# Where the maxima of the FP4 down weight are taken, where the first LoRA factors are split, and a rounding factor moved into a product

## The reference

```
x = x + norm(x) @ (weight * blockmask).T                     # 512 x 512, fp32
x = x + norm(x) @ (int4 weight * scale).T + bias             # 512 x 512
z = norm(x)                                                  # NF4 block with LoRA (rank 16), FI = 1792
  x1 = z + o((q(z) + k(z) + v(z)) / 3)
  x  = x + x1 + down(silu(gate(x1)) * up(x1))                # each weight: NF4[codes] * scales + B @ A
z = norm(x)                                                  # NVFP4 block, 1376 features
  h = silu(fp4(z) @ fp4(gate).T) * (fp4(z) @ fp4(up).T)
  x = x + fp4(h) @ fp4(down).T * mlp_output_scale + z @ lr_A @ lr_B

def fp4(w):                                                  # after a permutation of the channels
    s  = max(max(abs(w)) / (448 * 6), 1e-12)                 # one scale of the whole tensor
    sb = clip(max over 16 of abs(w / s) / 6, 1e-12, 448)     # one scale of each block of 16
    return sign(w) * fp4_level(abs(w / s / sb)) * sb * s     # the last 128 channels pass unquantized
```

## Time and profile before

| | |
|---|---|
| median of 3 runs | 788.04 us (787.42 to 793.67) |
| profiled execution, its own time | 790.65 us |
| its span | 789.3 us |
| its mean granted TensorE clock | 0.972 |
| TensorE busy | 704.4 us (89%) |
| VectorE busy | 555.6 us (70%) |
| ScalarE busy | 447.5 us (57%) |
| GpSimd busy | 219.2 us (28%) |

### The profile page before, as it was taken

How to read it: one execution, slowest core, us unless ns; L and a number is a source line. 1 busy time by engine, 2 the same in 40 slices (tenths; PEclk the granted TensorE clock), 3 DMA queues, 4 the chain that set the end, 5 groups by cost and what they waited for, 6 DMA issues and landing times.

```text
span 789.3 us, 10753 instructions
## 1 busy us (share of the span) xinstructions
PE 704.4 (89%) x3832; PEld 528.2 (67%) x3832; DVE 555.6 (70%) x1065; ACT 447.5 (57%) x579; POOL 219.2 (28%) x208
## 2 busy tenths in 40 slices
PE   1798766897999999999998998988999999989998
PEld 1465433575777766667675676765777789967886
DVE  6879986555577678798798975668543534487883
ACT  3767868576778687886776712354432211244552
POOL 1004100003355546647477564211401000000000
PEclk9999977898999999999999999999999999989999
DMA  9636578786557677676775211201301111100001
GB/s 348 193 116 202 187 236 263 237 282 221 173 168 252 187 243 261 214 248 200 245 220 176 105 37 34 61 28 40 107 26 38 26 38 39 53 1 14 27 27 41
DMA packets 55541, 110.79 MB, mean 140 GB/s; under 512 B 9904, under 2 KB 20560, under 8 KB 55232
## 3 DMA queue, kind: packets, MB, share of 16 engines
q1 hardware_dynamic: 42912, 80.28, 31.5%
q0 software_dynamic: 4384, 14.09, 6.1%
q10 hardware_dynamic: 8192, 15.73, 5.8%
HBM read 92.19 MB, written 17.89 MB: 139 GB/s over the span
## 4 chain that ended last, share of the span: by engine, by line
PE 49%; DVE 20%; ACT 10%; DMA 8%; issue 8%; SPq 3%; ACTq 1%; POOL 0%; DVEq 0%; POOLq 0%
PE bank L1246 13%; PE bank L1247 13%; PE bank L1248 13%; ACT hot L1668 3%; DMA rep<-codes 3%; DMA wide_buf<-in_down_flat 2%; DVE x L2035 2%; DVE hot L1924 2%; PE bank L1360 2%; PE bank L1558 1%; ACT c L1628 1%; DVE bank L1950 1%; DVE q_a L1999 1%; DVE stats L1845 1%; SPq L2328 1%
## 5 line engine op out<-in xcount | busy, mean ns | idle before, releaser
L1668 ACT ACTIVATE hot<-rep,levels 128x2048 f16<-128x2048 f16 x94 | 192.9, 2092 | 24.5 <-DMA rep<-codes 14.7
L1246 PE MATMUL bank<-zt_h,w_h 128*128 128x512 f32 (+1 forms) x232 | 93.7, 404 | 3.2 <-DVE zt_l L2023 2.0
L1248 PE MATMUL bank<-zt_h,w_l 128*128 128x512 f32 (+1 forms) x232 | 91.3, 394 | 0.0
L1247 PE MATMUL bank<-zt_l,w_h 128*128 128x512 f32 (+1 forms) x232 | 91.3, 393 | 0.0
L1246 PE MATMUL bank<-w_h,xq_h 128*128 128x512 f32 (+1 forms) x192 | 74.0, 385 | 2.2 <-ACT xq_l L1760 1.9
L1247 PE MATMUL bank<-w_l,xq_h 128*128 128x512 f32 (+1 forms) x192 | 71.9, 374 | 0.0
L1248 PE MATMUL bank<-w_h,xq_l 128*128 128x512 f32 (+1 forms) x192 | 71.8, 374 | 0.0
L1360 PE MATMUL bank<-hot,diag 128*32 128x512 f16 x856 | 60.7, 394 | 9.2 <-ACT hot L1668 8.4
L2179 POOL TENSOR_TENSOR q_a<-q_a,q_m 128x384 f32<-128x384 f32 (+3 forms) x34 | 35.8, 1052 | 69.9 <-DVE q_m L1809 69.8
L1924 DVE TENSOR_SCALAR hot<-rep,levels 128x2048 f16<-128x2048 f16 x56 | 52.3, 933 | 4.0 <-DMA rep<-codes 3.9
L1962 DVE TENSOR_TENSOR w_l<-bank,w_h 128x512 fp32r<-128x512 f32 x46 | 31.7, 689 | 31.8 <-ACT w_h L1676 31.5
(11 more groups left out here) (221 smaller groups left out, 1676.5 us busy)
## 6 DMA issues: line engine op xcount, KB each, us to landing
rep<-codes SPq DMA_DIRECT2D x56, 512.0 KB, 5.3
...
raw<-in_codes_gu_t ACTq DMA_DIRECT2D x14, 512.0 KB, 4.9
...
raw<-in_codes_attn_t ACTq DMA_DIRECT2D x7, 512.0 KB, 4.3
raw<-in_codes_down_t ACTq DMA_DIRECT2D x7, 512.0 KB, 6.3
...
wide_buf<-in_gate_flat SPq DMA_DIRECT2D x5, 512.0 KB, 5.4
```

Source lines behind the costliest of these rows:

```text
L1246: PE.matmul(psum, lh, rh, start=first, stop=False, **kw)
L1247: PE.matmul(psum, lh, rl, start=False, stop=False, **kw)
L1248: return PE.matmul(psum, ll, rh, start=False, stop=last, **kw)
L1668: S.activation(hots[plan.slot[hot_ring(t), (t, m)]][:], codes_in_place(t), ACT.Relu, bias=levels[:, at:at + 1], scale=levels[:, at + 1:at ...
```

## The change

- **Maxima of down.** The generator of the maxima is split: `gm_steps("early")` takes gate and up where all 18 were taken before, with its own last reduction and its own maximum over the partitions. `gm_steps("down")` (eight steps: one for the first two loads, six reductions, one for the last reduction) runs inside `fp4_weights`, between the rounding of chunk 1 and that of chunk 2 of up, in `wide_buf`, which is free from the last transpose of up's chunk 1 on. The first gather of down, which was asked for one chunk earlier, comes behind it and waits for its last reduction. `gm_clamp` is done once for gate and up and once for down.
- **The rate** of the FP4 side goes from 0.8 to 0.88.
- **The first LoRA split**, `stacks(0)`, moves from ahead of the planes of the first tile to behind those of the third.
- **The factor** 1 + 2^-22 behind each reciprocal is taken out there, and applied in the product that uses the reciprocal: `scalar_tensor_tensor(out, src, TIES_UP, reciprocal, mult, mult)` in place of `tensor_tensor(out, src, reciprocal, mult)`, for the weights, x and h.

The diff, cut to its core:

```diff
@@ -183,11 +184,13 @@
 ATT_RATE = 1.0
 NF4_RATE = 0.86
 MAX_RATE = 1.0
-FP4_RATE = 0.8
+FP4_RATE = 0.88
 CHUNKS = [(f, min(512, FF - f)) for f in range(0, FF, 512)]
 PER = FF * D // P
 GM_PARTS = [(c, min(2 * D, PER - c)) for c in range(0, PER, 2 * D)]
 GM_ALL = [(name, i) for name in ("gate", "up", "down") for i in range(len(GM_PARTS))]
+GM_RANGES = {"early": (0, 2 * len(GM_PARTS)), "down": (2 * len(GM_PARTS), 3 * len(GM_PARTS))}
+GM_COLUMNS = {"early": slice(0, 2), "down": slice(2, 3)}
 HN = NT // 2
 AHEAD = tuple((NG - 1, n) for n in range(HN, HN + 3))
 SCALED_AT = {(0, 0): (0, 1), (0, 2): (1, HN), (HN - 1, 0): (HN, NT)}
...
@@ -420,7 +423,6 @@
         cast(1)
         ship(1)
         fetch(2)
-        stacks(0)
         hits(0)
         yield
         tiles = 2 * len(jobs)
...
@@ -442,6 +444,8 @@
             low_parts()
             if t + 1 < tiles:
                 hits(t + 1)
+            if t == 1:
+                stacks(0)
             if t and u == 0:
                 if i > 1:
                     stacks(i - 1)
...
@@ -474,26 +478,30 @@
 
     ready_nf4 = ready_batches()
 
-    def maxima():
-
-        p.add("idx")
-        p.sends("idx_in", "idx", 3)
+    def gm_steps(part):
+        n0, n1 = GM_RANGES[part]
 
         def load(n):
-            if n < len(GM_ALL):
+            if n < n1:
                 p.add("gm_load", *GM_ALL[n])
                 p.sends(f"wide_in{n % 2}", ("gm", *GM_ALL[n]))
 
-        load(0)
-        load(1)
+        load(n0)
+        load(n0 + 1)
         yield
-        for n in range(len(GM_ALL)):
-            if n:
+        for n in range(n0, n1):
+            if n > n0:
                 load(n + 1)
             p.add("gm_max", *GM_ALL[n])
             yield
-        p.add("gm_all")
+        p.add("gm_all", part)
         yield
+
+    def maxima():
+
+        p.add("idx")
+        p.sends("idx_in", "idx", 3)
+        yield from gm_steps("early")
 
     def fp4_weights():
         def gather(n):
...
@@ -512,6 +520,9 @@
         pending = None
         for n, (name, c) in enumerate(STREAM):
             outer = OUTER[name][c]
+            if (name, c) == ("up", len(CHUNKS) - 1):
+                yield from gm_steps("down")
+                gather(n + 1)
 
             def turn(o):
                 p.add("wturn", name, c, o)
...
@@ -522,10 +533,10 @@
             for o in range(outer):
                 if o + 1 < outer:
                     turn(o + 1)
-                else:
+                elif n + 2 != STREAM.index(("down", 0)):
                     gather(n + 2)
-                if n == o == 0:
-                    p.add("gm_clamp")
+                if o == 0 and (name, c) in (("gate", 0), ("down", 0)):
+                    p.add("gm_clamp", "early" if name == "gate" else "down")
                 p.add("wround", name, c, o)
                 p.note("wread", name, c, o)
                 p.take("q_tmp", 2, ("w", name, c, o), ("pool", "wfinish", name, c, o))
...
@@ -1794,13 +1805,6 @@
             steady.wait_ge()
             return V.tensor_scalar(lo, lo, 1e-12, None, ALU.mult)
 
-        def reciprocals(r, c):
-
-            steady.up(V.reciprocal(r, c))
-            steady.wait_ge()
-            steady.up(V.tensor_scalar(r, r, 1.0 + 2.0 ** -22, None, ALU.mult))
-            steady.wait_ge()
-
         def magic(ua, um, nq):
 
             steady.up(V.tensor_scalar(um[:, 0:nq].bitcast(U32), ua[:, 0:nq].bitcast(U32), 0x7F800000, 0x00400000,
...
@@ -1966,12 +1970,14 @@
                 V.tensor_reduce(gm[:, n:n + 1], wide_buf[:, n % 2 * 2 * D:n % 2 * 2 * D + w], AX, ALU.max,
                                 apply_absolute_value=True).then_inc(sem("gm_max_dve"), 1)
             elif kind == "gm_all":
-                dve.wait_ge(*done("dve", "gm_max", *GM_ALL[-1]))
-                V.tensor_reduce(gm_own, gm[:, 0:len(GM_ALL)].rearrange("p (w i) -> p w i", w=3), AX,
+                (n0, n1), cols = GM_RANGES[key[0]], GM_COLUMNS[key[0]]
+                dve.wait_ge(*done("dve", "gm_max", *GM_ALL[n1 - 1]))
+                V.tensor_reduce(gm_own[:, cols], gm[:, n0:n1].rearrange("p (w i) -> p w i", i=len(GM_PARTS)), AX,
                                 ALU.max).then_inc(sem("gm_all_dve"), 1)
             elif kind == "gm_clamp":
-                dve.wait_ge(*done("pool", "gm_all"))
-                steady.up(least_scale(gm_of, gm_lo))
+                cols = GM_COLUMNS[key[0]]
+                dve.wait_ge(*done("pool", "gm_all", *key))
+                steady.up(least_scale(gm_of[:, cols], gm_lo[:, cols]))
                 steady.wait_ge()
             elif kind == "wround":
                 name, c, o = key
...
@@ -1993,10 +1999,12 @@
                 w3 = STREAM.index((name, c)) // len(CHUNKS)
                 steady.up(V.tensor_scalar(cb, rb, 1.0 / 6.0, gm_lo[0:orow, w3:w3 + 1], ALU.mult, ALU.max))
                 steady.wait_ge()
-                reciprocals(rb, cb)
+                steady.up(V.reciprocal(rb, cb))
+                steady.wait_ge()
                 if name == "down":
                     V.tensor_scalar(cb, cb, mscale[:, o:o + 1], None, ALU.mult)
-                ins = V.tensor_tensor(blocks_of(ua, nq), blocks_of(src, nq), spread_of(rb, orow, nq), ALU.mult)
+                ins = V.scalar_tensor_tensor(blocks_of(ua, nq), blocks_of(src, nq), TIES_UP, spread_of(rb, orow, nq),
+                                             ALU.mult, ALU.mult)
                 if nq == w:
                     ins.then_inc(sem("wread_dve"), 1)
                     dve.wait_ge(*done("dve", "wread", *key))
...
@@ -2107,9 +2116,7 @@
                 dve.wait_ge(*done("pe", "allcol", what))
                 steady.up(least_scale(turn(("all", what))[:, P:P + 1], lo))
                 steady.wait_ge()
-                steady.up(V.reciprocal(inv_lo, lo))
-                steady.wait_ge()
-                V.tensor_scalar(inv_lo, inv_lo, 1.0 + 2.0 ** -22, None, ALU.mult).then_inc(sem("floor_dve"), 1)
+                V.reciprocal(inv_lo, lo).then_inc(sem("floor_dve"), 1)
             elif kind == "scale":
                 what, n0, n1 = key
                 lo, inv_lo = low_of[what]
...
@@ -2127,8 +2134,8 @@
                     dve.wait_ge(*done("dve", "hfin", key[2], key[1]))
                 for m in vacant("q_tmp", key):
                     dve.wait_ge(*m)
-                V.tensor_tensor(blocks_of(ua, nq), blocks_of(src, nq), spread_of(r, P, nq), ALU.mult).then_inc(
-                    sem("round_dve"), 1)
+                V.scalar_tensor_tensor(blocks_of(ua, nq), blocks_of(src, nq), TIES_UP, spread_of(r, P, nq), ALU.mult,
+                                       ALU.mult).then_inc(sem("round_dve"), 1)
             elif kind == "qturn":
                 src, w, nq, c, r = fp4_source(key)
                 ua, um, _, _ = q_tmp[plan.slot["q_tmp", key]]
...
@@ -2203,20 +2210,24 @@
                 pool.wait_ge(*done("act", "norm", 1, n))
                 G.tensor_tensor(x[:, n, :], x[:, n, :], bias16, ALU.add).then_inc(sem("biased_pool"), 1)
             elif kind == "gm_all":
-                pool.wait_ge(*done("dve", "gm_all"))
-                G.partition_all_reduce(gm_of, gm_own, P, bass.bass_isa.ReduceOp.max).then_inc(sem("gm_all_pool"), 1)
+                cols = GM_COLUMNS[key[0]]
+                pool.wait_ge(*done("dve", "gm_all", *key))
+                G.partition_all_reduce(gm_of[:, cols], gm_own[:, cols], P, bass.bass_isa.ReduceOp.max).then_inc(
+                    sem("gm_all_pool"), 1)
             elif kind == "gather":
                 name, c = key
                 n, fw = STREAM.index(key), CHUNKS[c][1]
                 wide = wide_bufs[n % 2]
                 pool.wait_ge(*landed("idx"))
-                if n >= 2:
+                if key == ("down", 0):
+                    pool.wait_ge(*done("dve", "gm_max", *GM_ALL[-1]))
+                elif n >= 2:
                     then_name, then_c = STREAM[n - 2]
                     pool.wait_ge(*done("pe", "wturn", then_name, then_c, OUTER[then_name][then_c] - 1))
                 elif n:
                     pool.wait_ge(*done("pe", "merge_mm", KD - 1))
                 else:
-                    pool.wait_ge(*done("dve", "gm_max", *GM_ALL[-1]))
+                    pool.wait_ge(*done("dve", "gm_max", *GM_ALL[GM_RANGES["early"][1] - 1]))
                 if name == "down":
                     for t, rows in row_tiles(c):
                         gather(wide[0:rows, t * D:(t + 1) * D], a["down_t"],
...
@@ -2335,6 +2346,8 @@
                 n, (c0, w) = GM_ALL.index(key), GM_PARTS[i]
                 if n < 2:
                     sp.wait_ge(*done("dve", "int4_mul", 1, 1))
+                elif n - GM_RANGES["down"][0] in (0, 1):
+                    sp.wait_ge(*done("pe", "wturn", "up", 1, OUTER["up"][1] - 1))
                 else:
                     sp.wait_ge(*done("dve", "gm_max", *GM_ALL[n - 2]))
                 SP.dma_start(wide_buf[:, n % 2 * 2 * D:n % 2 * 2 * D + w], a[name + "_flat"][:, c0:c0 + w]).then_inc(
```

20 lines of the change are left out of this document (11 added, 9 removed).

## The result

The changed kernel takes 795.72 us in the median of 20 runs (790.15 to 799.24), the kernel before 789.86 us on the same chips. The ratio is 1.0068, with an interval of 1.0046 to 1.0090: 5.4 us slower, where 3.8 us faster was forecast. The profiled execution has a span of 797.2 us (789.3 before) and a mean granted clock of 0.957 (0.972 before). It took 798.5 us by its own time, 2.8 us more than the median, so its rows show 2 to 3 us more of loss than the ratio does.

The account below looks back on a forecast made before the run. TensorE was taken as what must be kept fed, other engines' time counting only where a matmul waits. Terms -2.0 - 4.2 + 3.0 - 0.6 = -3.8 us took 788.04 us to 784.2 us, range 774 to 794 us.

Parts of the forecast that it names:

- the LoRA split put off: At the start: ScalarE's first NF4 ramp can begin at 20.07 us, 2.0 us gained, bounds 0 and 3.5.
- the factor, a third of 7.1 in the loop, and the tail: Loop roundings: 7.1 us less on VectorE, a third let through; last block's tail: 0.6 us gained.
- the maxima leave the attention: Attention products: TensorE's 2.67 us wait for zt_l and 1.5 us of slow clock go, 4.2 us gained.
- the maxima in the loop, a third of 16.4: NF4 loop: six down reductions add 6.6 us of work and 9.8 us of waits to VectorE, a third let through.
- the test that the prediction set for itself: Wrong if the attention's first product comes no earlier, or TensorE's idle time from 330 to 380 us grows over 5 us.
- a third comes through: NF4 loop: of VectorE's 9.3 us more, a third reaches TensorE, 3.0 us lost.
- D: Rival, chance 0.13: the loop's maxima decide, six waits of 2.6 us all felt, kernel slower at 796.3 us.
- B: Rival, chance 0.26: everything carries, and the loop gains 2.5 us as roundings pause during the maxima: 777.2 us.
- C: Rival, chance 0.15: early gains of 6.2 us are absorbed by the loop, which still loses 3.0 us: 790.4 us.

Follow-up runs that it names:

- down_left_out: early_both with the down maxima left out altogether (six loads, six reductions), the floor of the down scales taken from up's maximum: ratio 0.9918 to the kernel before.
- no_reduce: The changed kernel without GpSimd's maximum over the partitions for down, loads and reductions kept: ratio 1.0023 to the kernel before.
- second_reduce: The kernel before with one more GpSimd maximum over the partitions ahead of the first down gather, result unused: ratio 1.0101.
- reduce_only: The changed kernel without down's loads, reductions and eight steps, one unused maximum over the partitions kept: ratio 1.0071 to the kernel before, 0.9936 without that maximum.
- factor_only: The kernel before with only the factor 1 + 2^-22 moved into the product: ratio 0.9947, median 785.99 us.
- stacks_only: The kernel before with only the first LoRA split put behind the third tile's planes: ratio 0.9964, median 787.24 us.
- rate_only: The kernel before with only the FP4 rate raised from 0.80 to 0.88: ratio 1.0043.
- reductions_only: The changed kernel without the six down loads and the second maximum over partitions, the six reductions kept: ratio 1.0006 to the kernel before.
- early_both: The kernel before with the LoRA split put off and the factor in the product, maxima left where they were: ratio 0.9897, median 782.20 us.

## Why the prediction was wrong

The prediction's terms, with the loop's third and the tail set down by part, and 790 us for the ratios:

| step | forecast, us | measured, us |
|---|---|---|
| the LoRA split put off | -2.0 | -2.8 (-5.0 to -0.7) |
| the factor, a third of 7.1 in the loop, and the tail | -3.0 | -4.2 (-6.9 to -1.5) |
| the maxima leave the attention | -4.2 | -2.4 (-4.7 to 0) alone; none seen beside the other two |
| the maxima in the loop, a third of 16.4 | +5.5 | +11.9 (1.0068 less 0.9918) |
| sum | -3.8 | +5.4 |

The measured terms do not add one by one. The first three together are down_left_out, -6.5 us, and -6.5 + 11.9 = +5.4 us. The last term also holds the rate and the eight steps.

**The start** was right in kind and size: the ramp came at 21.45 us (near 20 was said), the events behind came 1.7 us earlier, and the attention's first product came at 140.04 us (139.6 was said). What limits the shift was another transfer than the one named.

**The factor** was right: the forecast lies within the interval. The product costs what it did (0.56 us in both forms at 128x384), so what remains is one instruction less for each of the roundings.

**The attention** failed at one sentence, "What is late next is the handover to the first gate product at 195 us, which is unchanged." It was not unchanged. TensorE arrived earlier, ScalarE's 4.08 us of ramps ahead of zt_h did not (185.87 against 185.65 us), because the ramps before them waited 4.86 us for a spread of codes, and the wait of 2.00 us became 4.17 us. The delay of the spreads was named in the prediction, with a term of 0 as its outcome, and charged nothing. The first gate product came at 191.80 us, not near 189.

**The loop is the step that failed.** The waits for the loads were forecast as 9.8 us and measured as 8.1, the reductions as 6.6 us and found so, and TensorE's idle time from 330 to 380 us grew by only 2.2 us, so the test that the prediction set for itself was passed, but it looked at the wrong place. (The traffic of "208" GB/s, which the prediction took for this part, is that of 345 to 430 us; from 330 to 380 us the kernel before moved 239 GB/s.) What was too small is the term itself, +5.5 us before the factor's share, where +11.9 us were measured. Two things were missing in it.

- The term for the loop put GpSimd's second maximum over the partitions at nothing. The prediction named "on GpSimd the first down gather and the roundings behind it", but as waiting for the last reduction, not for the reduction's own standstill. By no_reduce it is 3.6 us of the 11.9, by second_reduce 8 us and by reduce_only 10.7 us where it stands alone. The trace of before gave no more than a hint. Its only such reduction, at 187.11 us, is followed by eight gathers and then by 8.18 us without work until 206.39 us, but ScalarE's at_h, which the next instruction needs, was ready only at 205.45 us, so just the last 0.94 us stand without a reason. Where at_h came sooner the standstill shows by itself: 7.11 us in factor_only, 7.24 in stacks_only and 7.55 in rate_only, with nothing to wait for. It cost nothing there, since no rounding had begun. Timeline of the kernel before, GpSimd, behind that reduction and behind gathers alone:

```profile
206.39 1.28 POOL L2241 TENSOR_TENSOR at_l<-ztok,at_h 128x512 fp32r<-128x512 f32 x1 [8.18 <-ACT at_h L1700]
...
368.26 0.95 POOL L2173 DMA_INDIRECT wide_buf<-in_down_t,down_idx  x1 [0.30 <-issue]
369.22 1.02 POOL L2179 TENSOR_TENSOR q_a<-q_a,q_m 128x384 f32<-128x384 f32 x1
```

- The rule "a third comes through" had no row behind it. In the traces, what comes through is set by whether an addition to x or a scale that TensorE needs stands behind a rounding of VectorE. Six reductions and the pause in the roundings (reductions_only, +5.5 us for 6.6 us of work) cost nearly the whole of that work, at 396 and 447 us, 20 and 70 us behind the reductions. That is the larger part of the +11.9 us. And nearly every standstill took a slow clock with it, which no term of the loop had: 0 us from 300 to 500 us before, 6 us after.

**The rivals.** D's time (796.3 us) is nearly the one measured (795.7 us), but by luck: the six waits that it charged whole at 2.6 us were three of 8.1 us in all, and nothing was lost at them. B falls with the sign, and C with stacks_only and early_both, whose gains were not absorbed. The last down rounding began at 490.9 us, not near 481, and the multiplication by the factor behind each reciprocal is gone, as said.

**Open.** What the idle time ahead of and behind GpSimd's maximum is made of; whether the six reductions or the pause of eight steps in the roundings makes the 5.5 us; whether the gathers delayed the spreads in the attention; and why the rate moves the time as it does. Nor was it tried to make the maximum over partitions otherwise. The kernel does that already for the quantized x, with a transpose on TensorE (545.30 us in the kernel before), a reduction on VectorE (545.68 us) and a way back that ends at 546.5 us. But no_reduce, which has no such maximum for down at all, is still 1.3% behind early_both, so it would not save the move.
